# The order of the first loads, and the last batch's second part of the block in two halves of 256 queries

## The reference

```python
def attn(x):                       # (4, 512, 128), 16 heads, head width 8
    q, k, v = split(x @ qkv_w.T + qkv_b)
    a = softmax(q @ k.T * 8**-0.5)
    return (a @ v) @ fc_w.T + fc_b + x
def ffn(x):                        # hidden width 512, weights in {-1, 0, 1} times a scale per row
    h = silu(x @ w1.T * s1) * (x @ w2.T * s2)
    h = gelu(h @ h1.T * sh1)
    h = gelu(h @ h2.T * sh2)
    return h @ w3.T * s3
x = layernorm(x + attn(x))
x = layernorm(x + ffn(x))
```

## Time and profile before

| what | value |
|---|---|
| median of 3 runs (lowest, highest) | 379.07 us (378.65, 379.9) |
| the profiled execution's own time | 380.18 us |
| its span in the trace | 378.4 us |
| PE busy | 330.8 us, 87% of the span |
| DVE, ACT, POOL busy | 246.0, 246.9, 155.8 us |
| mean granted TensorE clock | 0.956 |

### The profile page before, as it was taken

How to read it: one execution, slowest core, us unless ns; L and a number is a source line. 1 busy time by engine, 2 the same in 40 slices (tenths; PEclk the granted TensorE clock), 3 DMA queues, 4 the chain that set the end, 5 groups by cost and what they waited for, 6 DMA issues and landing times.

```text
span 378.4 us, 5154 instructions
## 1 busy us (share of the span) xinstructions
PE 330.8 (87%) x1625; PEld 152.8 (40%) x1650; DVE 246.0 (65%) x482; ACT 246.9 (65%) x427; POOL 155.8 (41%) x231
## 2 busy tenths in 40 slices
PE   5267879999999999999999989989989996968981
PEld 3164212222334443434444524535634441446750
DVE  4416877787778987777788787658678401044763
ACT  3314675676767787768976887676688788664320
POOL 9045992000004476000881456625389607017101
PEclk9778899999999999999999999999999998987996
DMA  4944200211221121202102302030000100000001
GB/s 99 276 123 98 33 28 3 43 23 21 45 36 38 29 39 19 35 11 42 31 0 37 49 2 44 11 61 14 17 2 1 29 3 0 1 2 0 6 23 31
DMA packets 21903, 13.29 MB, mean 35 GB/s; under 512 B 6771, under 2 KB 20723, under 8 KB 21875
## 3 DMA queue, kind: packets, MB, share of 16 engines
q1 hardware_dynamic: 21427, 12.53, 16.0%
q10 hardware_dynamic: 448, 0.39, 0.4%
HBM read 5.38 MB, written 1.05 MB: 17 GB/s over the span
## 4 chain that ended last, share of the span: by engine, by line
PE 67%; issue 8%; ACT 7%; DVE 6%; POOL 5%; SPq 4%; ACTq 2%; DMA 1%; POOLq 0%; DVEq 0%
PE f_bank L413 16%; PE pv_bank L453 16%; PE s_bank L426 13%; PE st_bank L437 12%; DVE negmax L757 3%; ACT prob L619 3%; PE f_bank L396 2%; SPq L379 2%; ACTq L331 2%; POOL hT L933 2%; ACT L619 1%; ACT h_nat L685 1%; PE st_bank L413 1%; PE f_bank L474 1%; DMA x_in<-in_L_attn_x_dram 1%
## 5 line engine op out<-in xcount | busy, mean ns | idle before, releaser
L757 DVE TENSOR_REDUCE negmax<-s_bank 128x1 f32<-128x512 f32 x256 | 167.3, 683 | 53.5 <-PE s_bank L426 52.5
L619 ACT ACTIVATE prob<-st_bank 128x512 f32<-128x512 f32 x256 | 141.4, 596 | 43.1 <-PE st_bank L437 32.1
L426 PE MATMUL s_bank<-stack 125*128 125x512 bf16 x256 | 93.3, 389 | 9.7 <-DVE negmax L757 5.5
L437 PE MATMUL st_bank<-stack 128*128 128x512 bf16 x231 | 83.6, 386 | 5.6 <-ACT prob L619 3.3
L453 PE MATMUL pv_bank<-prob,v_sb 128*32 128x512 f32 x512 | 73.0, 612 | 0.8 <-ACT prob L619 0.5
L413 PE MATMUL f_bank<-act,hT 128*128 128x512 f32 x208 | 66.5, 437 | 0.8 <-DVE act L832 0.6
L426 PEld LDWEIGHTS s_bank<-stack 125*128 125x128 bf16 x256 | 23.4, 98 | 71.5 <-DVE negmax L757 44.1
L437 PEld LDWEIGHTS st_bank<-stack 128*128 128x128 bf16 x256 | 23.6, 97 | 57.1 <-ACT prob L619 38.0
L921 POOL CAST mparts<-negmax 128x16 bf16<-128x16 f32 (+1 forms) x17 | 3.3, 196 | 98.6 <-DVE negmax L757 98.5
L413 PEld LDWEIGHTS f_bank<-act,hT 128*128 128x128 f32 x208 | 38.9, 190 | 10.6 <-issue 1.1
L967 POOL TENSOR_TENSOR act<-h_nat,act 128x512 fp32r<-128x512 f32 x24 | 30.1, 1277 | 0.3
(11 more groups left out here) (156 smaller groups left out, 387.4 us busy)
## 6 DMA issues: line engine op xcount, KB each, us to landing
stack<-parts SPq DMA_DIRECT2D x120, 48.0 KB
x_in<-in_L_attn_x_dram SPq DMA_DIRECT2D x4, 256.0 KB, 2.9
h_nat<-in_L_ffn_h_w_dram SPq DMA_DIRECT2D x1, 1024.0 KB, 8.4
work<-in_L_ffn_h_w_dram SPq DMA_DIRECT2D x1, 1024.0 KB, 9.9
x_res<-in_L_attn_x_dram SPq DMA_DIRECT2D x4, 256.0 KB, 2.7
out_dram<-y SPq DMA_DIRECT2D x4, 256.0 KB, 2.3
work<-in_L_ffn_w_w_dram SPq DMA_DIRECT2D x2, 256.0 KB, 4.8
stack<-parts ACTq DMA_DIRECT2D x8, 48.0 KB
```

The costliest lines, as they stand in the source:

```text
L426: nc.tensor.matmul(s_bank[n % NS][:, :], stack[0][0:MROW, h, qt * P:(qt + 1) * P], stack[1][0:MROW, h, :], start=True, stop=True).then_inc ...
L437: last = nc.tensor.matmul(st_bank[n % NST][:, to:to + nq], stack[1][:, h, kt * P:(kt + 1) * P], stack[0][:, h, q0:q0 + nq], start=True, st ...
L619: nc.scalar.activation(prob[:, n % NP, :], st_bank[n % NST][:, :], ACT.Exp, scale=SCALE).then_inc(ev_st, 1)
L757: nc.vector.tensor_reduce(negmax[:, g % 2, col:col + 1], s_bank[n % NS][:, :], AX.X, ALU.max, negate=True).then_inc(ev_s, 1)
```

## The change

Two edits, and all five order strings are written anew.

**First loads.** The DMAs of w1/w2, of h1/h2 and of w3 become tokens (`lw`, `lh`, `l3`). x of batch 1 is now issued right behind fc_w, then w1/w2 and h1. h2 and w3 follow the spreading of batch 0, and `more` (fc_b and the scales) comes after the second `mrow`. PE transposes fc_w (`wf`) right behind the qkv weights and into s_bank 1, ahead of the projections. DVE adds the bias to v of batch 0 before it makes the second `r`. ACT copies out a weight block before x of batch 1. `w_raw` has a fourth buffer, the tile aT.

**The tail in two halves.** UNITS gets two entries for batch 3, tiles 0 and 1, then tiles 2 and 3. Every instruction of its output projection and second part is issued twice at half the width, and the hidden layers go first half, second half, layer by layer.

```diff
 SP_ORDER = """
-more xin xres xin zq*2 zk*4 zq*6 mrow*2 xin mrow spread ...
+xin lw lh xin zq*2 zk*2 zq zk*2 zq*3 mrow zq*2 lh l3 mrow*2 more xres spread ...
...
-    UNITS = [(b, 0, NT) for b in range(B)]
-    LU = len(UNITS) - 1
-    CU = 3
+    UNITS = [(b, 0, NT) for b in range(LAST)] + [(LAST, t0, 2) for t0 in (0, 2)]
+    CU, LT, TU = 3, LAST, len(UNITS) - LAST
...
-        w_raw = [m[:, :, :].rearrange("p t c -> p (t c)") for m in (x1[0], x1[1], res[1])]
+        w_raw = [m[:, :, :].rearrange("p t c -> p (t c)") for m in (x1[0], x1[1], res[1])] + [aT[:, :]]
...
         def h_piece(n):
-            if n < LU * 2 * HP:
+            if n < LT * 2 * HP:
                 return (n // (2 * HP), (n // HP) % 2, (n % HP) // NK, n % NK)
-            n -= LU * 2 * HP
-            return (LU, n // TAIL_HP, None, n % TAIL_HP)
+            n -= LT * 2 * HP
+            return (LT + (n // TAIL_HP) % TU, n // (TU * TAIL_HP), None, n % TAIL_HP)
+
+        def h_out(n):
+            if n < LT * 2 * NK:
+                return (n // (2 * NK), (n // NK) % 2, n % NK)
+            n -= LT * 2 * NK
+            return (LT + (n // NK) % TU, n // (TU * NK), n % NK)
...
-            for i, w in enumerate((w1_w, w2_w)):
-                sp.dma_start(w_nat[:, i, :, :], w.rearrange("(t p) c -> p t c", p=P)).then_inc(ld_w, 16)
-            sp.dma_start(h_nat[0], h1_w.rearrange("(t p) c -> p t c", p=P)).then_inc(ld_h, 16)
...
+                elif what == "lw":
+                    for i, w in enumerate((w1_w, w2_w)):
+                        sp.dma_start(w_nat[:, i, :, :], w.rearrange("(t p) c -> p t c", p=P)).then_inc(ld_w, 16)
+                elif what == "lh":
+                    sp.dma_start(h_nat[n], (h1_w, h2_w)[n].rearrange("(t p) c -> p t c", p=P)).then_inc((ld_h, ld_h2)[n], 16)
+                elif what == "l3":
+                    sp.dma_start(w3_nat, w3_w).then_inc(ld_w3, 16)
...
                 elif what == "wf":
                     pe.wait_ge(ld_fc, 16)
-                    nc.tensor.transpose(s_bank[0][:, 3 * P:4 * P], fc_nat, ident[:, :]).then_inc(ps_wq, 1)
+                    nc.tensor.transpose(s_bank[1][:, 0:P], fc_nat, ident[:, :]).then_inc(ps_wq, 1)
...
-                    pe.wait_ge((hi, lo)[halves[0]], kk + 1)
+                    pe.wait_ge((hi, lo)[halves[0]], NK * (u - LT) + kk + 1)
```

More of the change, by code:

```diff
@@ L8 @@
 SP_ORDER = """
-more xin xres xin zq*2 zk*4 zq*6 mrow*2 xin mrow spread mrow spread mrow spread mrow spread mrow xres spread mrow spread mrow spread mrow spread xres
-mrow spread mrow spread mrow spread mrow spread out mrow xres mrow out mrow out*2
+xin lw lh xin zq*2 zk*2 zq zk*2 zq*3 mrow zq*2 lh l3 mrow*2 more xres spread mrow xin spread mrow spread mrow spread mrow xres spread mrow spread mrow
+spread mrow spread mrow spread xres mrow spread mrow spread mrow spread out xres mrow*3 out*4
 """
@@ L18 @@
[L18 to L21, removed]
@@ L47 @@
+u*2 m gh gl gh gl gh gl gh gl u h0 l0 h0 l0 m h0 l0 h0 l0 p2 gh*4 gl*4 p1*2 gh gl gh gl gh gl gh gl p2*3
 """
@@ L669, in _ @@
                 elif what == "h":
-                    u, layer, k = n // (2 * NK), (n // NK) % 2, n % NK
+                    u, layer, k = h_out(n)
                     act.wait_ge(ps_h, n + 1)
@@ L675, in _ @@
                         else:
-                            act.wait_ge(*((lo_g, n) if u < LU else (lo_gt, NK)))
+                            act.wait_ge(*((lo_g, n) if u < LT else (lo_gt, NK * (u - LT + 1))))
                         wait(act, ps_w3T, before(u))
-                    nc.scalar.activation(raw[:, k, cols(u)], space(*h_first(u, layer, k))[:, 0:width(u)], ACT.Copy if u < LU else ACT.Gelu,
+                    nc.scalar.activation(raw[:, k, cols(u)], space(*h_first(u, layer, k))[:, 0:width(u)], ACT.Copy if u < LT else ACT.Gelu,
                                          scale=hs[:, 2 + layer, k:k + 1]).then_inc(emptied(*h_first(u, layer, k)), 1)
@@ L844, in _ @@
                     if k == 0:
-                        wait(dve, ps_h, 2 * NK * before(u) if layer == 0 else 2 * NK * u + NK)
-                    nc.vector.tensor_copy((act1, act2)[layer][0][:, k, cols(u)], raw[:, k, cols(u)]).then_inc(hi_g if u < LU else hi_gt, 1)
+                        wait(dve, ps_h, 2 * NK * before(u) if layer == 0 else 2 * NK * u + NK if u < LT else 2 * NK * LT + NK * (u - LT + 1))
+                    nc.vector.tensor_copy((act1, act2)[layer][0][:, k, cols(u)], raw[:, k, cols(u)]).then_inc(hi_g if u < LT else hi_gt, 1)
                 elif what == "gl":
-                    u, layer, k = CU + n // (2 * NK), (n // NK) % 2, n % NK
-                    a, m = (act1, act2)[layer], NK * layer + k + 1
-                    dve.wait_ge(*((hi_g, 2 * NK * u + m) if u < LU else (hi_gt, m)))
+                    n += 2 * NK * CU
+                    u, layer, k = h_out(n)
+                    a = (act1, act2)[layer]
+                    dve.wait_ge(*((hi_g, n + 1) if u < LT else (hi_gt, n + 1 - 2 * NK * LT)))
                     nc.vector.tensor_tensor(a[1][:, k, cols(u)], raw[:, k, cols(u)], a[0][:, k, cols(u)].bitcast(F32),
-                                            ALU.subtract).then_inc(lo_g if u < LU else lo_gt, 1)
+                                            ALU.subtract).then_inc(lo_g if u < LT else lo_gt, 1)
                 elif what == "wq":
```

72 lines of the change are left out of this document (37 added, 35 removed).

## The result

| | before | after |
|---|---|---|
| median of 5 runs each, one chip | 379.58 us (378.65 to 379.9) | 375.85 us (374.88 to 376.54) |
| ratio | | 0.9892, 95% interval 0.9873 to 0.9911 |
| span of the profiled execution | 378.4 us | 373.7 us |
| PE idle up to 60 us | 21.4 us | 16.0 us |
| PE idle in the middle | 12.0 us | 15.6 us |

By the ratio the change saves 4.1 us (1.08% of 379.6). The forecast was 9.5 us less than the median of before. In the traces of before, after and e12 every tenth record of a T is missing, the first included; the other traces have all 256.

The account below looks back on a forecast made before the run. PE at full clock bounds the middle, so gains come at the two ends, 35.6 us of idle: 380.18 - 6.5 (start) - 3.0 (tail) = 370.7 us, predicted 369.6 as the profiled execution was 1.1 above median; range 364 to 376.5.

Parts of the forecast that it names:

- The first loads: Start: x of batch 1 no longer waited for, fc_w wait 3.2 us added; gain 6.5 us, bounds 2 to 9.5.
- The rival of a start in part: Start: T early, but the maxima's path or h2 holds PE; gain shrinks to 2 us, 374 us; chance 0.18.
- The matmuls in halves: Batch 3's A, B, H, W: 176 matmuls of 256 columns at 0.125 us, 22.0 us, 2.0 us more.
- The rival of exposed loads: Batch 3's half matmuls cannot cover their weight loads: 33.4 us instead of 22.0, 381.0 us in all; chance 0.06.
- The chain of the tail: From batch 2's last hidden layers to the end, three parts: gain 0.6, loss 0.2, gain 1.7 us; whole tail gains 3.0.
- The first part: Tail, from the end of batch 2's hidden layers to batch 3's first: 12.4 us instead of 13.05, gain 0.6.
- The forecast's fourth piece: Before the tail's count begins: half the projection moves behind it and PE's 0.6 us idle fills; gain 0.9 us.
- The middle: Rewritten strings between the two ends: its 12.0 us of idle can give or cost perhaps 3 us, no sign put.
- the middle takes it back: Middle: new strings lose what the start won, S, T and P being bound by DVE and ACT; 379 us; chance 0.06.

Follow-up runs that it names:

- e12: Changed kernel's order up to 100 us, then the kernel before's middle to 322 us, tail in halves, fc_w's transposes as in the changed kernel; 371.33 us, ratio 0.9764.
- e2: Tail alone: order and first loads of the kernel before up to about 322 us, then the changed kernel's last batch in halves; 376.93 us, ratio 0.9924.
- e4: Start of the kernel before up to about 67 us, then the changed kernel's middle and tail in halves; 383.42 us, ratio 1.0094.
- e9: Changed kernel with one place of ACT's order altered: behind batch 1's Gelu, four exponentials go ahead of the copy `u`; 374.86 us, ratio 0.986.
- e10: Changed kernel with the four exponentials at the same place as in e9 put ahead of the Gelu too; 382.17 us, ratio 1.0057.
- e1: Start alone: changed kernel's order up to about 60 us, then the order of the kernel before, last batch in one piece; 375.81 us, ratio 0.9881.
- e3: Changed kernel's start up to about 60 us and its tail in halves, the order of the kernel before in between; 374.13 us, ratio 0.9831.
- e5: Changed kernel's order up to 140 us, then the order of the kernel before up to the last batch, in halves; 373.44 us, ratio 0.9818.
- e8: e5 (changeover of orders at 140 us) with PE's transposes of fc_w moved back behind v; 371.65 us, ratio 0.9779.
- e11: Changed kernel's order up to 100 us, the kernel before's middle to 322 us, tail in halves, fc_w's transposes moved behind v; 368.59 us, ratio 0.9691.
- e7: Changed kernel with only fc_w's transposes moved back behind v (DVE's copy behind the first `mid`); 373.2 us, ratio 0.9835.

## Why the prediction missed

- **The first loads: right.** Forecast 6.5 us. The new wait for fc_w is 3.57 us (forecast 3.2), the first score came at 23.67 (22.4), the first T at about 35.9 (34). Both came somewhat late, but the lead over before at P 128 is 7.3 us in after and 6.8 in e12; before's profiled execution was itself 1.1 us above its median, so 6 us is a fair figure. The first score missed by 1.3 us: ACT's spreading began at 19.0 where I had 18.1. The rival of a start in part is out: h2, issued at 36.78, is in place when PE transposes its first block at 46.80 without a wait.
- **The matmuls in halves: right.** Forecast 0.125 us for 256 columns, measured 0.120; the load of 128 columns is hidden. 176 of them are 21.1 us. The Trainium skill ("TensorE: Matmul & The Clock Gate", Back-to-back issue gap) gives 262 cycles for 256 columns, an estimate of 0.109 and 19.2 us; the trace lies between this and my figure, at the spacing of the loads. The rival of exposed loads is out.
- **The chain of the tail: right in sum.** 13.5, 15.9 and 10.7 us, forecast 12.4, 16.2 and 11.3: 1.9 us less than before, forecast 2.1. That the sum is so near is in part luck: one part too short, two too long. The first part was 1.1 us longer than forecast. The half clock from 341.9 to 345.3 is at most 0.3 of it, since e12, which had none there, took 13.2 (329.24 to 342.42). The forecast's fourth piece, 0.9 us won ahead of the count, does not show: from the last P to the end of batch 2's hidden layers there are 7.7 us in before, 8.0 in after and in e12. Even so the tail alone saves 2.9 us by the times (e2, 1.8 to 4.0), forecast 3.0.
- **The middle: here it failed.** The step reads "The rewritten strings reorder the middle too: its 12.0 us of idle can give or cost perhaps 3 us, and I put no sign on it", and the sum counted it as nothing. It costs 4.9 us (e12 against after), more than the 3 us allowed either way, and e4 shows the loss without the early start. An unsigned term of 3 was in truth the second largest of the sum. Of the rivals, "the middle takes it back" named the mechanism, and it had 0.06; it took back half. Its argument for was right, that a poor order makes DVE and ACT late.
- **Where the 4.9 us are.** About 3.6 us go at 277 to 286 us of after, by the count of PE's work. About one of these is ACT's copy ahead of the exponentials by e9's profile, though e9's time alone can't be told from after's. The rest I put down to PE's order, which has scores but no T and few first-layer matmuls while Gelu and two table loads hold ACT. This is argued from the traces of before and e10; no run changed PE's string at this place. What is shown is that all runs that keep before's order there (e1, e3, e5, e8, e11, e12) lose nothing. From there to H number 192 the lead falls from 3.7 to 2.6 us, another 1.1; no run took that stretch apart. How much of either loss is the half clock that follows a wait is open.

That the lead was lost because the middle absorbs any lead, which I held possible at first, is refuted by e12: it keeps 7.0 us up to H number 192.

## What to carry to other kernels

When a change rewrites an order as a whole, its unintended parts are a term of the sum: compare the orders at each place where an engine changes its function table or waits for a chain of short steps, and give that term a sign and a chance before relying on gains at the ends. Taking the new order up to a moment and the old one from there on tells the parts apart, provided that the seam lies where the two orders have done the same work on every engine: it cost 0.4 to 0.7 us at 100 us (e12 against after, e11 against e7), 2.6 at 140, and a whole stall at 275. Nothing that waits for a late load should stand ahead of work that doesn't need it: moving one transpose gave 2.2 us. And where one engine must be away from its usual work, as ACT for Gelu, see what the others' orders hold for that time.

## What I had not expected of the hardware

- At half width DVE's tensor operations took 0.42 us (128x256; 0.69 at 128x512), ACT's Silu 0.47 (0.69), and POOL's power for the layer norm 0.70 at 128x2 against 1.01 at 128x4: halving the width saves 30 to 40% of an instruction, not half. The last layer norm, timelines of DVE and POOL:

```profile
368.15 0.42 DVE L734 TENSOR_TENSOR res<-s_bank,x 128x256 f32<-128x256 f32 x1
...
370.38 0.60 DVE L756 TENSOR_SCALAR y<-res,mv,rstd 128x128 f32<-128x128 f32 x2 [0.81 <-POOL rstd L903]
...
369.65 0.70 POOL L903 TENSOR_TENSOR rstd<-rstd,mhalf 128x2 f32<-128x2 f32 x1 [2.06 <-DVE rstd L747]
```

- The early scores did not buy a full clock. TensorE was at 1.2 GHz for 13.7 us in one piece in after (24.5 to 38.1), e11 (22.0 to 35.7) and e12 (24.2 to 37.8), where before had three pieces (14.1 to 24.3, 31.1 to 34.5, 41.4 to 44.8). PE was busy for 10.2 us of the one piece and for 9.9 us of the three together, so the work done at half clock is about the same; I tried nothing against it.
